# Four transformer-like layers on one core: score slots in turn, and the first pass of the alibi layer ended earlier

## The reference, cut to what matters

```python
x = L0_attn_x                                  # 4 sequences x 512 tokens x 128
for layer in (0, 1, 2, 3):                     # state space, causal, rope, alibi
    xn = _layernorm(x, axis=-1)
    s = attn_ref[layer](xn)
    g = _silu(ffn_ref[layer](xn))              # mixtures of experts
    x = x + s * g

# layer 3, attention (16 heads of 8)
scores = jnp.einsum('bhid,bhjd->bhij', q, k) / scale
scores = scores + _alibi_bias(N_HEADS, seq_len, M_SLOPE, x.dtype)[None]
attn = jax.nn.softmax(scores, axis=-1)
out = jnp.einsum('bhij,bhjd->bhid', attn, v)
out = out.transpose(0, 2, 1, 3).reshape(batch, seq_len, d_model)
return out @ out_w.T + out_b

# layer 3, feed-forward: each of 16 experts takes its 160 best tokens of 2048
vals, idx = jax.lax.top_k(masked, cap)
xe = x_flat[idx]
h = jax.nn.gelu(jnp.einsum('ncd,ndh->nch', xe, W1) + b1[:, None, :])
out = jnp.einsum('nch,nhd->ncd', h, W2) + b2[:, None, :]
```

## Time and profile before

| | us |
|---|---|
| median of 3 runs | 1927.68 |
| lowest and highest | 1926.33, 1933.56 |
| the profiled execution | 1933.77 |
| its span in the trace | 1931.3 |
| in it, the alibi layer's first pass of sequence 0 ends | at about 1555 |
| the three turns | 1555 to 1857 |
| the last second pass and the end | 1857 to 1931.3 |

### The profile page before, as it was taken

The page is one execution under the profiler, slowest core; times in us unless marked ns, Lnnn a source line. Parts: engine busy times, 40 slices in busy tenths (PEclk is TensorE's granted clock), DMA queues, the critical chain, the costliest instruction groups (busy, mean ns, idle before and its releaser), DMA issues. The chain is left out here.

```text
span 1931.3 us, 23980 instructions
## 1 busy us (share of the span) xinstructions
PE 1562.3 (81%) x8656; PEld 782.9 (41%) x8656; DVE 1178.2 (61%) x2370; ACT 1016.9 (53%) x1658; POOL 208.8 (11%) x152
## 2 busy tenths in 40 slices
PE   5999999987798688977888778984785677877886
PEld 2556555554454344433444334432222322322442
DVE  4789999899846733367434665236216777675522
ACT  4787787774042167532675336662772123334675
POOL 1343342432000000000000000000000000001003
PEclk9999999999899799868899799886566567889988
DMA  4433232353110300203002020006012212022002
GB/s 163 119 78 76 78 80 74 83 182 77 60 51 17 99 18 1 82 1 99 19 1 82 17 82 19 17 1 203 25 33 77 71 35 76 14 65 58 1 2 71
DMA packets 91621, 116.30 MB, mean 60 GB/s; under 512 B 10096, under 2 KB 71536, under 8 KB 91120
## 3 DMA queue, kind: packets, MB, share of 16 engines
q1 hardware_dynamic: 89808, 110.05, 20.0%
q0 software_dynamic: 1696, 4.72, 0.8%
HBM read 83.27 MB, written 31.46 MB: 59 GB/s over the span
## 5 line engine op out<-in xcount | busy, mean ns | idle before, releaser
L1665 ACT ACTIVATE scratch<-ps 128x1024 f32<-128x1024 f32 x272 | 270.8, 1022 | 212.7 <-PE ps L1267 68.4
L2079 DVE TENSOR_REDUCE neg_max<-ps 128x2 f32<-128x1024 f32 (+2 forms) x224 | 234.4, 1068 | 106.5 <-PE ps L1211 105.5
L1648 ACT ACTIVATE ps<-ps 128x512 f32<-128x512 f32 x256 | 150.1, 586 | 84.4 <-PE ps L1257 84.0
L1936 DVE TENSOR_TENSOR_SCAN scratch<-scratch 128x512 f32<-128x512 f32 x128 | 159.5, 1286 | 2.7 <-ACT scratch L1619 2.4
L1844 DVE SCALAR_TENSOR_TENSOR gated<-tanh,ps 128x512 f32<-128x512 f32 x88 | 60.4, 687 | 144.0 <-ACT tanh L1547 143.9
L1547 ACT ACTIVATE tanh<-ps 128x512 f32<-128x512 f32 x88 | 52.3, 595 | 160.8 <-PE ps L992 160.5
L1311 PE MATMUL ps<-scratch,values 128*32 128x512 f32 (+3 forms) x1024 | 130.1, 600 | 3.0 <-ACT scratch L1665 1.5
L1027 PE MATMUL ps<-xnt,weights_even 128*128 128x512 f32 x256 | 125.8, 613 | 7.4 <-ACT gated L1530 6.6
L2259 POOL TENSOR_SCALAR variance_eps<-mean_var 128x4 f32<-128x4 f32 x20 | 5.3, 264 | 1006.8 <-DVE mean_var L1764 1006.8
L992 PE MATMUL ps<-xnt,weights_odd 128*128 128x512 f32 x176 | 111.8, 721 | 0.0
L1665 ACT ACTIVATE weights_even<-ps 128x1024 f32<-128x1024 f32 x64 | 65.1, 1023 | 81.0 <-PE ps L1274 77.2
(11 more groups left out here) (323 smaller groups left out, 2955.9 us busy)
## 6 DMA issues: line engine op xcount, KB each, us to landing
scratch<-state_rows SPq DMA_DIRECT2D x64, 512.0 KB, 4.8
scratch<-parts_scratch SPq DMA_DIRECT2D x288, 96.0 KB, 2.4
parts_scratch<-weights_even SPq DMA_DIRECT2D x168, 128.0 KB, 2.4
weights_odd<-in_l SPq DMA_DIRECT2D x8, 519.5 KB, 6.5
weights_even<-in_l SPq DMA_DIRECT2D x1, 4096.0 KB, 16.2
weights_odd<-in_l SPq DMA_DIRECT2D x1, 4096.0 KB, 13.9
parts_scratch<-gated SPq DMA_DIRECT2D x15, 128.0 KB, 2.4
slots_scratch<-head_out SPq DMA_DIRECT2D x5, 256.0 KB, 5.0
```

Source lines behind the costliest of these rows:

```text
L1648: ins = act.activation(bank, bank, ACT.Exp, accum_out=dens[:, j, h:h + 1])
L1665: act.activation(dst, src, ACT.Exp).then_inc(q[l, "exp_done"], 1)
L1936: dve.tensor_tensor_scan(hs[:, g, :], da[n % RING][:, g, :], ub[:, g, :], 0.0, ALU.mult, ALU.add)\
L2079: ins = dve.tensor_reduce(dst, ps[:, base:base + 2, col:col + n], AX.X, ALU.max, negate=True)
```

## The change

Two things change, both for layer 3. Each turn's first-pass units are spread among all but the last 20 items of `main`, so "mx" stands 20 items before its end and not 10. And `slot` looks up one table for all layers, in which score units take the slots in turn in the order of the list, whatever their kind. No instruction is added or removed.

```diff
@@ last_layer
         main = stream[begin[b - 1]:begin[b]]
-        cover = len(main) - 10
+        cover = len(main) - 20
         main = spread(main[:cover], a[b]) + [("mx", l, b, 0)] + main[cover:]
@@ program
         for what, l, b, n in steps:
-            if what in ("a", "b") and l in (1, 2):
+            if what in ("a", "b"):
                 slots[what, l, b, n] = len(slots) % 2
-                stage = units[l][1][n][0] if what == "b" else None
+                stage = units[l][1][n][0] if what == "b" and l < 3 else None
@@ program
         def slot(l, kind, b, u):
 
-            if l < 3:
-                return slots[kind, l, b, u]
-            if not (kind == "a" and b == 0 or kind == "b" and b == NB - 1):
-                return 0 if kind == "a" else 1
-            return u % 2
+            return slots[kind, l, b, u]
```

## The result

The changed kernel takes 1917.31 us in the median of five runs (1916.07 to 1922.44). The kernel before, run beside it, took 1931.23 (1926.33 to 1934.05). The ratio is 0.9942 with a 95% interval of 0.9925 to 0.9959, so the change gains 11 us by the ratio, or 14 by the difference of the medians. The forecast was 20.2. The direction is right and the time lies in the range, but the gain by the ratio is about half of what was worked out. The profiled execution took 1917.85 us, and its span is 1915.1 where it was 1931.3.

A forecast was written before the change was run, and what follows sets the result against it. VectorE's work and idle time were taken to bound mixed parts 1 and 2, TensorE and its waits mixed part 3. Terms -11.3 - 13.0 - 16.0 + 4.4 + 6.5 + 9.2 = -20.2 us gave 1908, range 1898 to 1918.

The forecast's parts named there:

- half of the 14.2 before reductions: Mixed part 1, first-pass units beside second-pass units: new slots halve VectorE's 14.2 us idle before reductions, leaving 16.6 of 23.7.
- an added wait costed at nothing: TensorE's queue: 39 of 96 second-pass units now wait for VectorE's reductions; cost taken as nothing.
- rival 2: Turns of layer 3: waits only change their name, VectorE's idle time stays; +3.7 us, 1931; chance 0.21.
- mixed part 2: Turn 2's stretch of first-pass beside second-pass units: VectorE work 63.0 plus idle 12.0 makes 75.0 us, -13.0.
- tail 2: Turn 2's last second-pass units, 12 instead of 6: 16.5 us instead of 10, +6.5.
- mixed part 3: Turn 3's mixed stretch, without ranking: 7 us of moved work and 9 us of waits go, -16.
- tail 1: Turn 1's last second-pass units, 12 instead of 6, with six rank products: 16.4 us instead of 12, +4.4.
- tail 3: Turn 3's last second-pass units, with moved experts and a head group: 24.2 us instead of 15, +9.2.
- Mixed part 1: Turn 1's stretch of first-pass beside second-pass units: VectorE work 62.1 plus idle 16.6 makes 78.7 us, -11.3.
- The pace of 1.22 us: Tails: second-pass units taking the slots in turn follow each other every 1.22 us, so 12 take 14.6 us.
- the maxima's trip: Maxima written to memory and read back at a turn's end: 6.4 us, hidden behind 9.8, 3.4 to spare.
- Rival 3: Slower: idle time stays and tails keep the old pace of 1.73 us a unit; +22 us, 1950; chance 0.09.

The follow-up runs named there:

- the second execution: The changed kernel itself, unaltered, run and profiled once more beside three other experiments; ratio 0.9946 to the kernel before.
- with the head: The changed kernel with the first two first-pass units of each turn put ahead of its first second-pass unit; ratio 0.9983 to the kernel before.
- 10, 10, 20: The changed kernel with the maxima turned 10 items ahead in turns 1 and 2 and 20 in turn 3; ratio 0.9893 to the kernel before.
- 10, 10, 10: The changed kernel with the maxima 10 items ahead in all three turns, so only the slots are changed; ratio 0.9919 to the kernel before.

## Why the prediction was right in kind and wrong in size

**The step that failed** is "Of its idle 23.7 us I take off half of the 14.2 before reductions", in the terms of mixed parts 1 and 2. It credits the new slots with idle time of VectorE. With the slots alone 13.1 and 13.7 of the 14.2 and 15.5 us remain, and unchanged mixed parts scatter between 12.2 and 14.2 and between 14.7 and 15.5. The gap of the earlier trace rows is real, but TensorE walks one queue for both passes: where it no longer waits for the slot of its kind ahead of a first-pass unit, it waits for the same reductions ahead of a second-pass unit (20.3 us before, 13.8 + 8.0 with the slots alone, 20.4 + 3.4 with the change, all in turn 2). In the prediction this stood as an added wait costed at nothing and as rival 2, at 0.21. For the waits for reductions rival 2 was right; for the waits for exponentials it was wrong, and it is there, in the tails above all (38.0 to 28.2 us), that the slots earn most of their 15.6 us.

**The term that it spoiled** is mixed part 2: -7.9 us measured, and -4.9 in the second execution, where -13.0 was forecast. That is 5.1 of the 6.7 us by which the turns came short. In the terms of the forecast its length is VectorE's work and idle time: 63.0 + 12.0 was forecast and 64.7 + 14.8 measured, so 2.8 us of the miss are idle time that stayed, and 1.7 are work, of which less moved out than four rank steps and a head group were priced at. Of the idle time before, 4.76 us stood ahead of the first reduction, where the slots have no say. The rest of the miss is tail 2 (+8.8, not +6.5), mixed part 3 (-13.8, not -16, by the work that moved and not by the waits) and tail 1 (+5.8, not +4.4), with tail 3 the other way (+5.7, not +9.2).

**Mixed part 1** came out at 78.1 us where 78.7 was forecast, but not for the reason given. The order alone gives 81.9, the slots alone 87.2. The prediction built the part from VectorE's work and idle time; experiments took 6.3 us of work off VectorE, and closed its longest gap in mixed part 2, without the length following. What moved less is TensorE's time without work: in mixed part 1 it is 18.7 us before, 16.5 with the slots alone, 17.0 with the change and 16.7 with the rank steps moved; in mixed part 2 it is 17.6, 16.8, 19.3, 17.9, and 18.7 with the head. Over every execution here it lies between 14.5 and 20.2 us in these two parts, while VectorE's idle time goes from 14.6 to 23.9: steadier, but not constant. A sum on TensorE, with some 10 us of its busy time leaving each part, comes nearer: -12.1 and -7.9 were measured, -11.7 and -4.9 in the second execution. That TensorE's queue is the pace is argued from this near constancy; no run doubled or removed TensorE's work by itself.

**The tails.** The order was called a gain whose cost is the tails, +20.1 us in all; +20.3 was measured (38.0 to 58.3), the best term of the forecast and partly so by luck, since its parts are off by +1.4, +2.3 and -3.5. The pace of 1.22 us about holds where the clock is full: tail 2 of the 10, 10, 20 kernel has six units in 7.6 us. Tails 1 and 2 of the change begin at half clock, on TensorE from the turning of the maxima of turn 2:

```profile
1730.70 1.01 PE L1215 MATMUL ps<-consts,neg_max 128*16 128x128 f32 x4 [1.69 <-DVE neg_max L2075]
...
1735.08 1.94 PE L1288 MATMUL ps<-scratch,values 128*32 128x512 f32 x8
...
1737.82 1.86 PE L1288 MATMUL ps<-scratch,values 128*32 128x512 f32 x8
...
1742.42 1.07 PE L1288 MATMUL ps<-weights_even,values 128*32 128x512 f32 x8
```

Value products take 1.94 and 1.86 us there and 1.07 later; the forecast took full speed. In tail 3 the clock is 1.00. Before the change its 14.9 us held waits that the slots removed (9.7 with the slots alone, where the forecast left 11.8), and it ran at a granted clock of 0.77; the two together are most of why tail 3 came out short.

**The net of the order.** The prediction let moved work cost less in the tail than it saved in the mixed part. With the new slots in place, the order takes 256.3 - 230.0 = 26.3 us off the mixed parts and adds 58.3 - 28.2 = 30.1 to the tails. That net of 4 us by itself is within noise (0.9919 against 0.9942). What is clear of it is that 10, 10, 20 is 9 us faster than the change: in turns 1 and 2 the order costs. The reading that fits is that second-pass units rode along in the mixed part nearly free, and in the tail each costs its full time while VectorE is idle.

**What held.** The reorder did not run into the maxima's trip. The margin was overstated, though: the second hop came 3.70 us behind the first, not 1.57, while the stack loads issued just ahead of it still kept the DMA engines 70% busy up to 1645, so about 2 us were to spare in turn 1 and not 3.4:

```profile
1640.73 2.69 SPq L2365 DMA_DIRECT2D scratch<-parts_scratch  x6
...
1643.46 0.43 SPq L2399 DMA_DIRECT2D max_scratch<-xnt_sequence  x1
...
1647.16 0.54 SPq L2403 DMA_DIRECT2D scratch<-max_scratch  x2
...
1651.17 0.29 PE L1246 MATMUL ps<-consts,scratch 128*128 128x128 bf16 x2
```

No transfer to the slots was reached early. Rival 3, the slower one, needs the old tail pace, and the order alone shows it: 21 us slower, where 22 was worked out. That agreement is luck: the tails cost 48.1 us and not 38.8, and the mixed parts gave 27.8 and not 16.4. Of the two rules of the Trainium skill, that of "Perfetto Trace Analysis", section Matmuls, holds: the tails, which have second-pass units only, went from 38.0 to 28.2 us by the slots alone. The result reported in "TensorE: Matmul & The Clock Gate", section "HAM oscillation", that double buffering gave nothing, does not carry over here.

## What to carry to other kernels

When two kinds of work share one in-order queue, removing a wait ahead of one kind counts only once you have looked at what the next item in the queue waits for; sum the waits by their releaser, not by the line that waits, and expect only those to go whose releaser has slack. Idle time of an engine that is not the pace is no reserve: look for the engine whose time without work stays put, and take the part's length from that one. And before moving work out of a crowded stretch, ask whether it rode along there free; here the best distance tried was the shortest that still hid all but 0.8 us of the transfer, 5 items instead of 10 or 20, for 27 us instead of 11.

## What the runs showed of the hardware

- The granted clock of one and the same code differs between executions, and the time with it: 0.74, 0.76 and 0.69 for one mixed part, at 78.1, 78.5 and 81.4 us; 0.76 and 0.83 for another, at 90.2 and 85.3.
- Tails 1 and 2 of the change began at half clock, but not by the wait of 1.7 us ahead of the turning alone. In tail 1 the granted clock had fallen by 1630.5, before that wait began (1631.5). With 10 items behind the maxima the same code and nearly the same wait gave full clock through tail 1 in one kernel (10, 10, 20; 1.92 us) and a fall to half clock 1.4 us behind the turning in another (10, 10, 10; 1.78 us).
- A small write and read back through memory is not one price: 1.57 us from the first hop to the second with the DMA engines 10% busy, 3.70 behind stack loads, 5.9 beside gathers that kept the DMA engines 45% busy.
- A change of ScalarE's function and back cost two table loads of 1.28 us around 1.25 us of work, with no further gap between them.
